# Bilinear recommender tower: turning gathered rows on VectorE from block 2 on, and a step's products in one group

## The reference, cut to what matters

```python
e = jnp.stack([tbl_0[ids[:, 0]], ..., tbl_39[ids[:, 39]]], axis=1)   # 2048 x 40 x 32
iidx, jidx = jnp.triu_indices(40, k=1)
z = jnp.einsum('bpd,pde,bpe->bp', e[:, iidx, :], bilinear_matrices, e[:, jidx, :])
h = jnp.concatenate([z, dense_ctx], axis=1)                          # 780 + 16
h = jnp.maximum(h @ W_top1 + b_top1, 0.0)                            # 512
h = jnp.maximum(h @ W_top2 + b_top2, 0.0)                            # 256
y = h @ W_top3                                                       # 1
```

## Time and profile before

| what | value |
|---|---|
| median of 3 runs | 1245.42 us (1243.78 to 1253.85) |
| the profiled execution, its own time | 1242.61 us |
| its span, first to last instruction | 1240.8 us |
| time outside the span | 1.8 us |
| mean granted TensorE clock | 0.81 of full |

### The profile page before, as it was taken

How to read it: one execution, slowest core, us unless ns; L and a number is a source line. 1 busy time by engine, 2 the same in 40 slices (tenths; PEclk the granted TensorE clock), 3 DMA queues, 4 the chain that set the end, 5 groups by cost and what they waited for, 6 DMA issues and landing times.

```text
span 1240.8 us, 31357 instructions
## 1 busy us (share of the span) xinstructions
PE 960.8 (77%) x14536; PEld 473.6 (38%) x14536; DVE 549.1 (44%) x602; ACT 173.9 (14%) x432; POOL 475.7 (38%) x510
## 2 busy tenths in 40 slices
PE   4226779877887778787796878887788878888998
PEld 3012334333443234343243443443334423344556
DVE  4004345423654336443264443553335623355783
ACT  3011001011101111021010211012101121012211
POOL 7755342445233452434523434225442264322000
PEclk9557677778887879778887777878888878788999
DMA  4005100010000100001000010000100000000000
GB/s 143 14 13 180 34 10 6 10 35 10 6 8 8 35 10 6 9 9 35 11 6 8 8 34 10 6 7 14 32 10 6 6 13 10 8 7 6 4 3 2
DMA packets 24035, 24.54 MB, mean 20 GB/s; under 512 B 11173, under 2 KB 21217, under 8 KB 23777
## 3 DMA queue, kind: packets, MB, share of 16 engines
q0 software_dynamic: 15872, 8.16, 4.4%
q1 hardware_dynamic: 7418, 13.87, 3.4%
q10 hardware_dynamic: 616, 0.51, 0.1%
HBM read 22.44 MB, written 0.06 MB: 18 GB/s over the span
## 4 chain that ended last, share of the span: by engine, by line
PE 71%; issue 15%; another core or an unknown queue 10%; ACT 1%; DVE 1%; DMA 1%; POOL 0%; DVEq 0%; ACTq 0%
PE Y L614 23%; PE ZL L634 21%; PE ZL L660 13%; PE H L590 8%; PE H L573 3%; ACT xcols L742 1%; PE Y L669 1%; DVE prod L866 1%; DMA rows<-tbl,idx 0%; POOL rows L543 0%; PE Y L590 0%; PE Y L678 0%; PE ZL L640 0%; DMA idx<-ids 0%
## 5 line engine op out<-in xcount | busy, mean ns | idle before, releaser
L543 POOL DMA_INDIRECT rows<-tbl,idx x496 | 474.3, 956 | 652.5 <-PE H L573 472.3
L866 DVE TENSOR_TENSOR prod<-Y,xcols 128x1024 f32<-128x1024 f32 x352 | 419.3, 1221 | 538.0 <-remote 347.7
L634 PE MATMUL ZL<-prod,sel 128*32 128x256 f32 x3200 | 325.3, 432 | 48.3 <-issue 43.1
L614 PE MATMUL Y<-xcols,mats 32*64 32x256 f32 x6400 | 313.1, 434 | 29.3 <-ACT xcols L742 12.7
L614 PEld LDWEIGHTS Y<-xcols,mats 32*64 32x64 f32 x6400 | 162.6, 148 | 179.8 <-issue 132.0
L634 PEld LDWEIGHTS ZL<-prod,sel 128*32 128x32 f32 x3200 | 120.3, 120 | 194.9 <-issue 158.7
L660 PE MATMUL ZL<-z,w_sb 128*32 128x256 f32 x1568 | 162.8, 421 | 31.6 <-issue 30.0
L590 PE MATMUL H<-one,parts 125*32 125x256 bf16 x1560 | 97.7, 318 | 80.1 <-issue 80.0
L742 ACT ACTIVATE xcols<-H 32x256 f32<-32x256 f32 (+3 forms) x217 | 81.6, 376 | 546.1 <-PE H L573 335.0
L660 PEld LDWEIGHTS ZL<-z,w_sb 128*32 128x32 f32 x1568 | 66.9, 120 | 99.2 <-issue 73.8
L590 PEld LDWEIGHTS H<-one,parts 125*32 125x32 bf16 x1560 | 51.3, 104 | 128.9 <-issue 126.7
(11 more groups left out here) (43 smaller groups left out, 160.3 us busy)
## 6 DMA issues: line engine op xcount, KB each, us to landing
rows<-tbl,idx POOLq DMA_INDIRECT x496
idb<-ids_turned SPq DMA_DIRECT2D x8, 768.0 KB
w_sb<-w SPq DMA_DIRECT2D x1, 1792.0 KB
mats<-m_wide SPq DMA_DIRECT2D x1, 1152.0 KB
mats<-m_wide SPq DMA_DIRECT2D x1, 960.0 KB
mats<-m_wide SPq DMA_DIRECT2D x1, 768.0 KB, 6.3
tab<-tbl SPq DMA_DIRECT2D x6, 112.0 KB
w_sb<-w SPq DMA_DIRECT2D x1, 512.0 KB
```

Of the source, the lines that this page charges most:

```text
L543: pool.indirect_dma_start(out=rows[:, slot, t, D * q:D * (q + 1)], out_offset=None, in_=tables[f], in_offset=bass.IndirectOffsetOnAxis(ap= ...
L614: last = pe.matmul(Y[2 * D * c:2 * D * (c + 1), bank, cols], mats[D * r:D * (r + 1), u * P + 2 * D * c:u * P + 2 * D * (c + 1)], xcols[D * ...
L634: last = pe.matmul(Z[D * q:D * (q + 1), :], sel[:, GF * (SPAN - 1 - o):GF * (SPAN - 1 - o) + 32], prod[:, (2 * s + bank_of(k, q) // 2) % P ...
L866: dve.tensor_tensor(prod[:, half, :, :].rearrange("p b (u c) -> p b u c", c=BLK), Y[:, pair:pair + 2, :].rearrange("p b (u c) -> p b u c", ...
```

## The change

1. From block 2 on (and wave 8 of block 1, which does not exist any more with the new `ALL_HOT`) no wave is turned on PE. DVE turns a wave in one instruction, in squares of 32 by 32 (`flip`), into one of 4 slots of a new tile `squares`, and SP places the squares in `xcols` with 16 DMAs of 32 partitions by 256 bytes (`place_squares`), 4 for each field. `FLIP_AT` says after which step's products DVE does it. PE and ACT wait for the last of these DMAs (`s_cols`) before the first step that needs the wave. POOL's wait for the slot of `rows` is now on `s_flip`.
2. The samples of a block stand in another order in all columns (by quarters, `by_square`), because squares leave them so; the turns of blocks 0 and 1, the dense inputs and the output follow.
3. `ALL_HOT` is (0, 1, 2, 4, 6): the third hot wave is looked up in three more blocks instead of being gathered.
4. `multiply` issues all 16 products of a step by slot, column half and row, waits once (2s - 1 DVE products done) and signals once; DVE's first product of a step waits for all of it.
5. SP's queue after the start is laid out by steps.

```diff
-ALL_HOT = (0, 4)
+ALL_HOT = (0, 1, 2, 4, 6)
+FLIP_RING = 4
+def mixed_at(k):
+    return k // PAIR - 2
+TURNED_LATE = 8
+def flipped(n, j):
+    return n > 1 or (n == 1 and j >= TURNED_LATE)
-    turns = [(n, j) for n in range(NB) for j in range(len(cold(n))) if ("turn", n, j) not in HEAD]
+    turns = [(n, j) for n in range(NB) for j in range(len(cold(n))) if not flipped(n, j) and ("turn", n, j) not in HEAD]
+START = 2700
+GATHERED, GATHER = 1500, 125
+PLACED = 900
+def flip_steps():
+    flips, total = [], 0
+    for n in range(NB):
+        for j, fields in enumerate(cold(n)):
+            total += BT * len(fields)
+            gs = {f // GF for f in fields}
+            first = min([need(fields)] + [max(mixed_at(k), 0) for k in MIXED if gs & {UNITS[u][0] for u in SLOTS[k]}])
+            flips.append((n, j, n * NS + first, GATHERED + GATHER * total))
+    at, now, v = {}, START, 0
+    for s in range(NB * NS):
+        for n, j, first, there in flips:
+            if first == s:
+                now = max(now, there + (PLACED if flipped(n, j) else 0))
+        while v < len(flips):
+            n, j, first, there = flips[v]
+            if flipped(n, j):
+                if s < (n - 1) * NS + 1 or (first > s + 1 and (there > now or s in at.values())):
+                    break
+                at[n, j] = s
+            v += 1
+        now += max(tensor_work(s), PRODUCTS)
+    return at
-        behind = max(behind, 0) + PRODUCTS - tensor_work(s)
+        behind = max(behind, 0) + PRODUCTS - tensor_work(s) + FLIP * list(FLIP_AT.values()).count(s)
...
+            def place_squares(v):
+                n, j = flips[v]
+                slot = v % FLIP_RING
+                sp.wait_ge(s_flip, v + 1)
+                if n > 1:
+                    sp.wait_ge(s_prod, 2 * (n - 1) * NS)
+                for f in cold(n)[j]:
+                    g, q = divmod(f, GF)
+                    for c in range(QUARTERS):
+                        sp.dma_start(xcols[D * q:D * (q + 1), n % 2, g, BT * D * c:BT * D * (c + 1)],
+                                     squares[D * c:D * (c + 1), slot, q, :, :]).then_inc(s_cols[slot], DMA)
...
-                ready = [max(PASS[key] for key in sources(n, g)) + 1 for g in groups(w)]
-                pe.wait_ge(s_free, max(ready))
-                if s > 1:
-                    pe.wait_ge(s_prod, 2 * s - 2)
-                for pair in range(2):
-                    if pair == 1 and s > 0:
-                        pe.wait_ge(s_prod, 2 * s - 1)
+                if passes_of(n, groups(w)) > 0:
+                    pe.wait_ge(s_free, passes_of(n, groups(w)))
+                seen = flips_of(n, {g for a in range(w) for g in groups(a)})
+                for v in flips_of(n, groups(w)):
+                    if v not in seen:
+                        pe.wait_ge(s_cols[v % FLIP_RING], cols_landed(v))
+                if s > 0:
+                    pe.wait_ge(s_prod, 2 * s - 1)
+                for half, k in enumerate(slots(w)):
+                    cols = slice(half * BLK, (half + 1) * BLK)
+                    for c in range(2):
+                        for r in range(GF):
...
+            def flip(v):
+                n, j = flips[v]
+                slot, k = v % FLIP_RING, wave_number(n, j)
+                dve.wait_ge(s_rows[k % RING], landed(n, j))
+                if v >= FLIP_RING:
+                    dve.wait_ge(s_cols[slot], cols_landed(v - FLIP_RING))
+                dve.transpose(squares[:, slot, :, :, :].rearrange("p q t s -> p (q t s)"),
+                              rows[:, k % RING, :, :, :].rearrange("p q t d -> p (q t d)")).then_inc(s_flip, 1)
             def products(n, w, h):
                 s = n * NS + w
-                dve.wait_ge(s_y, 2 * s + h + 1)
-                if h == 0 and s > 1:
-                    dve.wait_ge(s_added, s - 1)
+                if h == 0:
+                    dve.wait_ge(s_y, s + 1)
+                    if s > 1:
+                        dve.wait_ge(s_added, s - 1)
```

More of the change, by code:

```diff
@@ L401, in tower @@
         s_turned = sem("s_turned")
+        s_flip = sem("s_flip")
+        s_cols = [sem(f"s_cols{k}") for k in range(FLIP_RING)]
         s_free = sem("s_free")
@@ L432, in stage, with by_square, passes_of, flips_of @@
             return Y[:, 5 - at, 0:BLK] if at < len(HEAD) else H[:, 0:BLK]
+        def by_square(cols):
+            return cols.rearrange("p (c t s) -> p t c s", c=QUARTERS, t=BT)
         def wave_number(n, j):
             return sum(len(cold(a)) for a in range(n)) + j
[L437 to L444, removed]
+        def passes_of(n, gs):
+            turned = [PASS["turn", n, j] for j, wave in enumerate(cold(n))
+                      if not flipped(n, j) and any(f // GF in gs for f in wave)]
+            looked_up = [PASS["hot", n, i] for i in hot(n) if any(f // GF in gs for f in HOT[i])]
+            return max(turned + looked_up, default=-1) + 1
+        flips = list(FLIP_AT)
+        def flips_of(n, gs):
+            return [v for v, (a, j) in enumerate(flips) if a == n and any(f // GF in gs for f in cold(n)[j])]
+        def cols_landed(v):
+            return (v // FLIP_RING + 1) * GF * QUARTERS * DMA
         mixes = [(n, k) for n in range(NB) for k in MIXED]
@@ L507, in _ @@
             sp.dma_start(b2_sb[:, :], b2).then_inc(s_w, DMA)
[L508 to L511, removed]
+            for n in range(NB):
+                for w in range(NS):
+                    for a in range(2, NB):
+                        if HOT_AT[hot_count(a - 1) - 1] + 1 == n * NS + w:
+                            spread_ids(a)
+                    if n > 0 and w == 1:
+                        load_dense(n)
+                    for v in [v for v, wave in enumerate(flips) if FLIP_AT[wave] == n * NS + w]:
+                        place_squares(v)
             sp.wait_ge(s_tails, HJ)
@@ L537, in gather @@
                 if k >= RING:
-                    pool.wait_ge(s_turned, k - RING + 1)
+                    a = waves[k - RING]
+                    if flipped(*a):
+                        pool.wait_ge(s_flip, flips.index(a) + 1)
+                    else:
+                        pool.wait_ge(s_turned, k - RING + 1)
                 for f in cold(n)[j]:
@@ L572, in turn @@
                         q = f % GF
-                        last = pe.matmul(stage(at)[D * q:D * (q + 1), t * P:(t + 1) * P], rows[:, slot, t, D * q:D * (q + 1)],
+                        last = pe.matmul(by_square(stage(at)[D * q:D * (q + 1), :])[:, t], rows[:, slot, q, t, :],
                                          ident[:, :], start=True, stop=True, skip_group_check=True)
@@ L600, in multiply @@
                             pe.wait_ge(s_m[k], DMA)
-                ready = [max(PASS[key] for key in sources(n, g)) + 1 for g in groups(w)]
-                pe.wait_ge(s_free, max(ready))
-                if s > 1:
-                    pe.wait_ge(s_prod, 2 * s - 2)
-                for pair in range(2):
-                    if pair == 1 and s > 0:
-                        pe.wait_ge(s_prod, 2 * s - 1)
[L608 to L616, removed]
-                                                 skip_group_check=True)
-                    last.then_inc(s_y, 1)
@@ L885, in _ @@
                         rest(*rests[5])
+                    for v in [v for v, wave in enumerate(flips) if FLIP_AT[wave] == n * NS + w]:
+                        flip(v)
                     for v in [v for v, s in enumerate(HOT_AT) if s == n * NS + w]:
```

32 lines of the change are left out of this document (23 added, 9 removed).

## The result

The changed kernel takes 1308.66 us (median, 1303.03 to 1312.41), the kernel before beside it 1249.63: a ratio of 1.047, 95% interval 1.040 to 1.054. It is slower by 59 us where 29 us less was forecast. The profiled execution has a span of 1307.3 us.

A forecast was written before the change was run, and what follows sets the result against it. Bound by PE's work plus 1.15 us for each gather. From 1242.6: -27.4 + 8.9 - 21.1 + 3 + 10 - 3 = 1213.0, plus 2.8 for the runs' median: 1216 us, range 1195 to 1235 (chance 0.62).

The forecast's parts named there:

- fewer gathers, more look-ups: Blocks 1, 2 and 6: 24 gathers fewer at 1.14 us, -27.4 us; 27 look-up places more at 0.33, +8.9.
- turns off PE, flips, order: 48 turns fewer on PE at 0.44 us, -21.1; 45 flips on DVE, +3; new multiply order and signals, -3.
- waiting for the columns: PE waiting for late placed columns, mainly blocks 3 and 7: +10 us (3 to 25).
- Placing: SP's 16 issues a wave at 0.43 us, 308 us in all, cost nothing on an idle queue except late columns, +10.
- Rival C: SP's small DMAs hold PE back beside gathers: 2.8 us for each of 45 stretches, 126 us, 1342 us total; chance 0.08.
- sign point: Rival C's cost a wave above which the change turns slower: 0.65 us.
- rival D: Turned waves cost PE nothing before, lying where gathers held PE back; the 21.1 us gain is missing: 1237 us; chance 0.08.
- rival B: The PE-DVE-PE chain becomes the bound; one-piece steps take 2.95 us instead of 2.50: +33 us, 1249 us; chance 0.10.
- The order: multiply by slot with one wait and one signal: -6 for order, +3 for block 0, together -3 us (-23 to +33).
- A: Rival: multiply's order fills all array tiles at once, 1.07 us falls to 0.86; 35 us faster, 1181 us; chance 0.12.
- Flips: 45 DVE transposes of 128x256 fp32 at 0.4 us each, costing +3 us (0 to 11).
- The bounds: All terms at their low bounds give about 1178 us, at their high ones about 1250.

The follow-up runs named there:

- list alone: Kernel before with only ALL_HOT = (0, 1, 2, 4, 6): ratio 0.983, 20.7 us less; 0.991 where the kernel before takes 691 us.
- nothing placed: Changed kernel without the 720 placement DMAs and the waits for them: ratio 0.982; 0.970 where the kernel before takes 691 us.
- 16 nobody waits: Changed kernel without placing, but 16 idle-tile DMAs a wave nobody waits for; ids, dense inputs on ACT's queue: 1.026; 1.104 where the kernel before takes 691 us.
- five DMAs a wave: Changed kernel placing each wave by one DMA to memory and one back per field, instead of 16: 0.991; 1.000 where the kernel before takes 691 us.

## Why the prediction was wrong

By ratios of the held condition, times 1249.6 (each measured row but the first is a difference of two runs, and their intervals allow some 10 us either way):

| step | forecast, us | measured, us | from |
|---|---|---|---|
| fewer gathers, more look-ups | -18.5 | -20.7 | list alone |
| turns off PE, flips, order | -21.1 | -1.5 | nothing placed, less the list alone |
| 16 DMAs a wave, nobody waits | 0 | +54.6 | 16 nobody waits, less nothing placed |
| waiting for the columns | +10 | +26.3 | changed kernel, less 16 nobody waits |
| sum | -29.6 | +58.7 | |

**Gathers and look-ups: right** in sum, with an interval of 7 us either way: 1.14 us a gather and 0.33 a place were measured together, not apart.

**Placing: the step that failed,** in both of its halves. "Where SP does nothing else" took an idle queue for a free one. Rival C named the mechanism, its sign point (0.65 us a wave, measured 1.2), and gave it 0.08; its price, 2.8 a wave, was too high, since PE's share of a stretch fell by a sixth (131 to 109 instructions) and not to nothing. The evidence held against C, ten DMAs at the start, was taken in a stretch without gathers, and block 7 above says that such a stretch can't show it.

The other half is the size of an issue, in the term of +10 us for late columns, which came to 26.3. The earlier trace rows gave 0.43 us for other DMAs; these start 0.63 us apart in the record's trace and take 10 to 12 us a wave instead of 6.8. Of the 26.3 us, block 7 has 13.5 and block 3 has 7.7 (175.6 against 167.9 with idle DMAs). Block 3's waits at steps 81 and 83 were foreseen. That four and three steps don't do in block 7 was foreseen too, but with 0.5 and 3.0 us. There the forecast also took SP's queue as free whenever a flip ends: with 10 to 12 us a wave it is not, and it starts on the flips of steps 177 and 180 only 2.7 and 5.4 us after they end.

**Turns: the second miss.** The earlier trace rows priced a turn in a gather-free stretch, but few turns stand there (in block 2 the 65 gathers, 1.25 us apart, fill some 80 of 151 us). The whole package of turns, flips and order gave 1.5 us (the intervals of the two runs allow some 10 either way); in the free condition the same difference, 0.991 to 0.970, is 14.7 us. Two causes are open. One is rival D: beside gathers PE is held anyway. In terms of blocks 1 to 6, the work fell by 17 us and the time over it rose by 28, for the same 342 gathers (list alone against nothing placed). The other is seen in the trace: beside gathers DVE starts late as well. Two rows of the kernel before, the first in a stretch of gathers (842.3 to 851.9) and the second just behind it, and four of the kernel with nothing placed:

```profile
847.91 0.69 DVE L856 TENSOR_TENSOR prod<-Y,xcols 128x512 f32<-128x512 f32 x1 [3.78 <-remote]
...
853.61 0.69 DVE L856 TENSOR_TENSOR prod<-Y,xcols 128x512 f32<-128x512 f32 x1 [4.41 <-remote]
```

```profile
872.05 1.12 PE L700 MATMUL Y<-xcols,mats 32*64 32x256 f32 x32
...
879.74 0.95 POOL L626 DMA_INDIRECT rows<-tbl,idx  x1 [0.30 <-issue]
...
882.50 2.36 DVE L963 TENSOR_TENSOR prod<-Y,xcols 128x1024 f32<-128x1024 f32 x2 [9.41 <-remote]
...
883.88 2.01 PE L700 MATMUL Y<-xcols,mats 32*64 32x256 f32 x32 [2.84 <-DVE prod L963]
```

PE's products are there at 873.2, the last gather ends at 880.7, and DVE starts at 882.5. With two signals DVE starts at least one product in each of the 38 stretches of the kernel before (later than 2.5 us behind the first gather); with one it starts none in 25 of the 35 of the kernel with nothing placed (counted from the records). PE then waits for it behind the gathers: 13 times, 18.3 us in all, against once and 0.7 us before. That is rival B in another place than it was looked for, beside gathers and not in gather-free steps. The 18.3 us are near the missing 20, but how much of that time PE could have used is not shown, and with idle DMAs the same wait is only 5.3 us in a slower kernel. The order alone was run only in the free condition, where it costs nothing; in the held one it wasn't tried, so how much of the missing 20 us is B and how much D stays open.

**The order** (A): no gain in the free condition; gather-free two-piece steps take 2.91 us against 2.94 in both conditions. **Flips:** 434 ns, near the 0.4 us taken.

**The bounds.** Added up as they stand in the prediction, the low ones give 1183 us and the high ones, with the 33 of the order, 1282, not 1178 and 1250. The 1309 measured lie beyond both, since the sum had no term for what DMAs do to PE.

## What to carry to other kernels

A queue that idles is not free: before small DMAs are added, ask what else runs in the stretch where they will fall, and price them by a row from that stretch, not from a quiet one. Price work that is taken away in the same manner, where it stands. Count issues as well as bytes: 16 DMAs of 8 KB a wave cost 16 x 0.63 us of a queue, five larger ones over a detour through memory were better in both conditions, and the one part of this change that pays in both is the shortest: three more entries in a list.

## What the runs showed of the hardware that was not expected

**One kernel, two times.** The same kernel takes 691 or about 1245 us; one chip showed 692 and, 17 minutes later, 1235. Gathers take 0.96 to 0.97 us each in both, and gather-free steps with two pieces 2.9 us. What differs is that beside eight or nine gathers PE starts some 140 instructions in 10 us in the one and 440 in the other, and with it the mean granted clock, 0.81 against 0.98. What switches it no run shows. A ranking made in the one needn't hold in the other: five DMAs a wave are 1.000 and 0.991, the changed kernel 1.165 and 1.047.

**Small DMAs of SP make this hold-back worse,** by 1.2 us a wave for 16 of 8 KB, with no data in common and no wait, and cost nothing in a block without gathers. The Trainium skill, Runtime: NRT & Kernel Launch, Instruction fetch mechanics, says that an engine's instructions are streamed by DMA; late instructions would fit "issue" growing with DMA work. But the traces do record transfers of kind "instruction", 16 KB each, and these are no slower where PE is held: behind 100 us they take 1.10 us on average beside gathers and 1.09 away from them in the kernel before, 1.09 and 1.11 with 16 idle DMAs a wave, and 1.10 beside gathers in the free condition. Whether one is asked for late no row shows. What holds PE back stays open.
